# Routing of a token group moved from six steps behind the attention loop to four, and the one-hot weighting moved from GpSimd to VectorE

## What is computed

```python
h = layernorm(x) @ W.T + b_W
e = (h @ a1)[:, None] + (h @ a2)[None, :] + b_a
e = where(e > 0, e, 0.2 * e)
attention = softmax(where(adj > 0, e, -9e15), axis=1)      # 2048 x 2048
x = x + attention @ h
z = layernorm(x)
logits = z @ Wr + br
topk_logits, topk_idx = top_k(logits, 2)
gates = softmax(topk_logits)
out = 0
for e in range(64):
    y = relu(z @ W1[e] + b1[e]) @ W2[e] + b2[e]            # 128 -> 256 -> 128
    out = out + combine[:, e:e+1] * y                      # combine: the gates at topk_idx, 0 elsewhere
x = x + out
```

## Time and profile before

| what | us |
|---|---|
| runs, median of 3 | 335.87 |
| runs, lowest and highest | 334.42 and 335.96 |
| the profiled execution | 333.78 |
| its span, first to last instruction | 332.0 |
| DVE busy | 216.4 |
| PE busy | 223.2 |
| POOL busy | 185.0 |
| ACT busy | 143.9 |

### The profile page before, as it was taken

One profiled execution on the slowest core, in us unless ns is written; L12 is line 12 of the kernel. 1 busy time (PEld: TensorE's weight loads), 2 busy tenths in 40 slices (PEclk: granted clock), 3 DMA queues, 4 the chain that ended last, 5 costly groups with the idle time before them and its releaser, 6 DMA issues.

```text
span 332.0 us, 6227 instructions
## 1 busy us (share of the span) xinstructions
PE 223.2 (67%) x1797; PEld 212.2 (64%) x1797; DVE 216.4 (65%) x583; ACT 143.9 (43%) x313; POOL 185.0 (56%) x210
## 2 busy tenths in 40 slices
PE   0790888999589579793431510209999999999830
PEld 0760788989589478793320410209999989999830
DVE  3859999999999299756734000005666756676476
ACT  1146858888862477632500200015664333444400
POOL 5510068998779867887774777773234323333300
PEclk9997899999989859998555585558999999999995
DMA  6993505998976200010111632213555656664184
GB/s 162 158 183 66 102 0 94 287 248 217 238 197 190 105 17 2 24 34 25 48 48 37 180 88 64 56 40 105 162 155 160 179 147 172 170 178 136 34 243 137
DMA packets 29056, 40.55 MB, mean 122 GB/s; under 512 B 3744, under 2 KB 24416, under 8 KB 28000
## 3 DMA queue, kind: packets, MB, share of 16 engines
q1 hardware_dynamic: 23280, 25.14, 25.7%
q0 software_dynamic: 5376, 14.72, 20.0%
q10 hardware_dynamic: 368, 0.30, 0.5%
HBM read 43.27 MB, written 5.26 MB: 146 GB/s over the span
## 4 chain that ended last, share of the span: by engine, by line
PE 35%; DVE 20%; issue 18%; POOL 14%; DMA 4%; ACT 4%; another core or an unknown queue 4%; SPq 1%; DVEq 0%; POOLq 0%; ACTq 0%
PE bank L907 13%; PE bank L917 13%; POOL table L361 7%; DVE arena L570 6%; DVE xs L753 2%; POOL ve L341 2%; POOL rstd L343 2%; PE bank L785 2%; DMA xs<-in_x 2%; DMA arena<-result 1%; POOL rk L369 1%; PE bank L897 1%; PE bank L822 1%; PE bank L775 1%
## 5 line engine op out<-in xcount | busy, mean ns | idle before, releaser
L907 PE MATMUL bank<-arena 128*128 x380 | 61.4, 287 | 30.3 <-issue 19.8
L907 PEld LDWEIGHTS bank<-arena 128*128 128x128 f32 x380 | 52.2, 200 | 31.7 <-issue 31.5
L407 POOL DMA_INDIRECT result<-arena x32 | 30.8, 963 | 60.8 <-DVE arena L731 55.9
L487 ACT ACTIVATE arena<-bank,arena 128x128 f32<-128x128 f32 x95 | 34.9, 368 | 60.9 <-PE bank L907 31.5
L822 PE MATMUL bank<-arena 128*128 128x130 f32 x512 | 61.3, 278 | 0.0
L822 PEld LDWEIGHTS bank<-arena 128*128 128x128 f32 x512 | 59.9, 194 | 0.0
L917 PE MATMUL bank<-w2s,arena 128*128 x380 | 59.1, 279 | 1.0 <-issue 1.0
L731 DVE SCALAR_TENSOR_TENSOR arena<-bank,arena 128x128 f32 x95 | 33.3, 351 | 39.6 <-PE bank L917 21.8
L812 PE MATMUL bank<-ident,arena 128*128 128x128 f32 x256 | 36.0, 301 | 25.9 <-DVE arena L570 25.4
L724 DVE TENSOR_SCALAR arena<-bank,arena 128x128 f32<-128x128 f32 x95 | 33.1, 348 | 30.2 <-issue 16.1
L917 PEld LDWEIGHTS bank<-w2s,arena 128*128 128x128 f32 x380 | 51.0, 195 | 1.6 <-issue 1.6
(11 more groups left out here) (156 smaller groups left out, 268.8 us busy)
## 6 DMA issues: line engine op xcount, KB each, us to landing
arena<-in_w1b SPq DMA_DIRECT2D x95, 129.0 KB
arena<-in_adj POOLq DMA_DIRECT2D x16, 512.0 KB, 6.9
w2s<-in_w SPq DMA_DIRECT2D x8, 1024.0 KB
arena<-result SPq DMA_DIRECT2D x8, 256.0 KB, 4.4
xs<-in_x SPq DMA_DIRECT2D x4, 256.0 KB, 5.4
out<-xs SPq DMA_DIRECT2D x4, 256.0 KB, 2.3
table<-rows_out,pos POOLq DMA_INDIRECT x32
arena<-table,arena POOLq DMA_INDIRECT x32
```

The costliest lines, as they stand in the source:

```text
L487: act.activation(hT[:, p % UH, 0, :], hp(p, 0), ACT.Relu, bias=w1s[:, p % UW, HID:HID + 1]).then_inc(e_ha, 1)
L907: ins = pe.matmul(hp(p, b), w1s[:, p % UW, P * b:P * b + P], xT_all[:, bass.ds(column, P)], start=True, stop=True)
```

## The change

Five things are altered. (1) The places of the routing in each engine's loop: PE's `route_a` goes from step z+2 behind `attend` to step z+1 ahead of `attend`, `route_b` from z+3 to z+1 behind `attend`, `route_c` from z+4 to z+2; DVE's `top2` from z+5 to z+3 and its `place` from z+6 to z+4; POOL's `counts` from z+5 to z+3, and its scatters from z+6 to z+4 on, with one tile a step for groups 0 and 1 in place of two. (2) ACT's `norm(s-3)` stands ahead of `evac(s-1)` in every step. (3) The groups have 4, 4, 4, 2 and 2 tiles. (4) POOL's `combine` is gone. DVE makes `comb` with 32 operations on 128x64 behind the table's last operation, with one 64-wide half for each of a token's two experts, so that the last transposes and products are 128 deep in place of 64, and `b2` is loaded twice. (5) `up(0)` stands ahead of `take(2)`.

```diff
-    START = [0, 4, 8, 11, 14, T]
+    START = [0, 4, 8, 12, 14, T]
-    SLOT = [0, GRP, 0, 3, 6]
+    SLOT = [0, GRP, 0, GRP, 6]
...
-        combT = carve(N)[0:E, :]
+        combT = carve(N)
+        comb = carve(T * TOPK * E).rearrange("p (t k e) -> p t k e", t=T, k=TOPK)
-        b2_s = sb("b2_s", [E, D])
+        b2_s = sb("b2_s", [TOPK * E, D])
-        idxf = sb("idxf", [P, GRP, TOPK])
+        idxf = sb("idxf", [P, T, TOPK])
...
 # POOL
-            def combine(q):
...
-            for s in range(T + 7):
+            for s in range(T + 5):
                 if 0 <= s - 3 < T:
                     rstd_of(s - 3)
                 if s + 5 < T:
                     load(s + 5)
                 for q in range(NG):
                     z = START[q + 1]
-                    if s == z + 5 and q < COUNTED:
+                    if s == z + 3 and q < COUNTED:
                         counts(q)
                     for j in range(SIZE[q]):
-                        if s == z + 6 + (0 if z > T - 3 else (j + q // 2) // 2):
+                        if s == z + 4 + (j, j, max(0, j - 1), 0, 0)[q]:
                             place(q, START[q] + j)
-                    if q < 2 and s == z + 6:
-                        combine(q)
...
-            for q in range(2, NG):
-                combine(q)
 # ACT
-            for s in range(T + 7):
+            for s in range(T + 4):
                 if s < T:
                     scores(s)
+                if 0 <= s - 3 < T:
+                    norm(s - 3)
                 if 1 <= s <= T:
                     evac(s - 1)
-                if 0 <= s - 3 < T:
-                    norm(s - 3)
                 for q in range(NG):
+                    if s == START[q + 1] + 2:
+                        route_a(q)
                     if s == START[q + 1] + 3:
-                        route_a(q)
-                    if s == START[q + 1] + 5:
                         route_b(q)
 # DVE
                 if q >= 2:
-                    dve.wait_ge(s_comb, min(q - 1, 2))
+                    dve.wait_ge(s_cnt, min(q - 1, 2))
...
-                if 1 <= q <= 2:
-                    dve.wait_ge(s_comb, q)
...
-                    if s == START[q + 1] + 5:
+                    if s == START[q + 1] + 3:
                         top2(q)
-                    if s == START[q + 1] + 6:
+                    if s == START[q + 1] + 4:
                         place(q)
...
             dve.scalar_tensor_tensor(mask, hi, pidx[:, :], above, ALU.is_gt, ALU.mult).then_inc(s_mask, 1)
+            for t in range(T):
+                for k in range(TOPK):
+                    ins = dve.tensor_scalar(comb[:, t, k, :], iota_e, idxf[:, t, k:k + 1], gate[:, k, t:t + 1], ALU.is_equal, ALU.mult)
+            ins.then_inc(s_comb, 1)
 # PE
-            for s in range(T + 7):
+            for s in range(T + 3):
                 if s < T:
                     turn(s)
+                for q in range(NG):
+                    if s == START[q + 1] + 1:
+                        route_a(q)
                 if 1 <= s <= T:
                     attend(s - 1)
                 for q in range(NG):
+                    if s == START[q + 1] + 1:
+                        route_b(q)
                     if s == START[q + 1] + 2:
-                        route_a(q)
-                    if s == START[q + 1] + 3:
-                        route_b(q)
-                for q in range(NG):
-                    if s == START[q + 1] + 4:
                         route_c(q)
...
-            for b in range(3):
-                take(b)
+            take(0)
+            take(1)
             up(0)
+            take(2)
             up(1)
```

More of the change, by code:

```diff
@@ L35, in build @@
     TAB = PACK * WORDS
-    assert TAB <= P and NB <= 32 and E <= 64
+    assert TOPK * E == P and TAB <= P and NB <= 32 and E <= 64
     EPS = 1e-5
@@ L150, in build @@
         gate = sb("gate", [P, TOPK, T])
-        cm = rk
         nm2 = sb("nm2", [P, T])
-        comb = sb("comb", [P, T, E])
         bank = [ctx.enter_context(nc.psum_tensor(f"bank{i}", [P, 512], F32)) for i in range(8)]
@@ L414, in _ @@
             act.dma_start(bss[:, :], biases.to_broadcast([P, D + 1 + E])).then_inc(d_small, 16)
-            act.dma_start(b2_s[:, :], b2).then_inc(d_small, 16)
+            for k in range(TOPK):
+                act.dma_start(b2_s[k * E:(k + 1) * E, :], b2).then_inc(d_small, 16)
             for b in range(4):
@@ L498, in _ @@
                 act.wait_ge(s_ct, q + 1)
-                act.activation(combT[:, START[q] * P:START[q + 1] * P], bank[q][0:E, 0:SIZE[q] * P], ACT.Copy).then_inc(s_cts, 1)
+                act.activation(combT[:, START[q] * P:START[q + 1] * P], bank[q][:, 0:SIZE[q] * P], ACT.Copy).then_inc(s_cts, 1)
         @block.vector
@@ L536, in _ @@
             stats(1)
-            dve.wait_ge(d_small, 16 * 3)
+            dve.wait_ge(d_small, 16 * 4)
             dve.tensor_copy(a2rep[:, :], a_s[:, 1:2].to_broadcast([P, P]))
@@ L595, in top2 @@
                 link(ins)
-                link(dve.tensor_copy(idxf[:, 0:n, :], idx8[:, 0:n, 0:TOPK]))
+                rows = slice(START[q], START[q + 1])
+                link(dve.tensor_copy(idxf[:, rows, :], idx8[:, 0:n, 0:TOPK]))
                 if q >= 2:
-                    dve.wait_ge(s_comb, min(q - 1, 2))
+                    dve.wait_ge(s_cnt, min(q - 1, 2))
                 for k in range(TOPK):
@@ L601, in top2 @@
                                             iota_e[:, :].rearrange("p (g e) -> p g e", g=1).to_broadcast([P, n, E]),
-                                            idxf[:, 0:n, k:k + 1].to_broadcast([P, n, E]), ALU.is_equal)
+                                            idxf[:, rows, k:k + 1].to_broadcast([P, n, E]), ALU.is_equal)
                 link(ins)
@@ L622, in place @@
                 link(dve.tensor_reduce(rank[:, :, 0:n], rk[:, :, 0:n, :], AX.X, ALU.add))
-                link(dve.scalar_tensor_tensor(posf[:, :, 0:n], idxf[:, 0:n, :].rearrange("p g k -> p k g"), float(N),
+                link(dve.scalar_tensor_tensor(posf[:, :, 0:n], idxf[:, rows, :].rearrange("p g k -> p k g"), float(N),
                                               rank[:, :, 0:n], ALU.mult, ALU.add))
@@ L649, in _ @@
             dve.wait_ge(s_pool, 4)
-            for s in range(1, T + 7):
+            for s in range(1, T + 5):
                 if s < T:
@@ L942, in _ @@
             for q in range(NG):
-                pe.wait_ge(s_comb, q + 1)
+                pe.wait_ge(s_comb, 1)
                 for g in range(SIZE[q]):
-                    ins = pe.transpose(bank[q][0:E, P * g:P * g + P], comb[:, START[q] + g, :], ident[:, :])
+                    ins = pe.transpose(bank[q][:, P * g:P * g + P], comb[:, START[q] + g, :, :].rearrange("p k e -> p (k e)"), ident[:, :])
                 ins.then_inc(s_ct, 1)
```

## The result

The changed kernel takes 344.38 us (median of 4 runs, 342.85 to 346.60), the kernel before 335.89 in the runs beside it: a ratio of 1.0263 [1.0232, 1.0294] (the two medians alone give 1.0253). The profiled execution took 344.34 against 333.78. The forecast was 350, range 330 to 358, slower.

The account below looks back on a forecast made before the run. DVE paces the loop at 6.13 us a step, barely ahead of a two-step dependence loop; delaying the first gather delays the end. 2.1 + 6.4 + 13.5 - 6.0 + 3.5 - 3.6 = +15.9 on 333.78: 349.7, said 350, range 330 to 358.

Parts of the forecast that it names:

- the two mechanisms: In the loop: norm ahead of `evac` lengthens plain steps, +6.4; PE waits for the norm ahead of `attend`, +13.5.
- the table: Stretch from the loop's end to the first gather: time left unchanged, 0, with bounds 0 and -8 us.
- First norm: At the first norm, already late, `evac`'s time ahead of the scores counts in full: +2.1 us.
- ACT's order: Norm ahead of `evac` puts `evac` inside the dependence loop: 0.8 us in about eight plain steps, +6.4.
- `route_a` ahead of `attend`: PE waits for the late norm before `attend`, delaying DVE by 2.5, 5.5 and 5.5 us in groups 0 to 2: +13.5.
- `combine` off POOL with spread scatters: In the step at 106.20, weighting and four scatters no longer hold back POOL's chain; L570's wait goes: -6.0 us.
- Third `top2`: With earlier routing a third group's `top2` is paid on DVE within the loop: +3.5 us.
- Behind the last `attend`: Earlier placing of the group on DVE, -2.0, and fewer scatters ahead on POOL, -1.6: together -3.6 us.
- Weights 0: 32 weight operations on DVE, at most 10 us, fit inside 40 us of standstill during the gathers: 0.
- the rival of up to +10: Weight operations on DVE hold up POOL's gathers, moving the last by 6.4 to 10.2 us: 356 to 360; chance 0.08.
- The faster rival: The norm is ready when PE finishes `turn`, so waits at `route_a` vanish and gains stay: 324 to 326; chance 0.20.
- the signs the forecast named: Plain steps over 6.5 us, waits before `route_a` and `residual`, last `attend` ending near 170, first gather near 194.

Follow-up runs that it names:

- the second chip: Changed kernel, unaltered, run again beside the kernel before on another chip (also called the repeat): 345.25 against 334.41 us, ratio 1.0322.
- the spreading: Kernel before with the weighting moved to DVE, plus scatters of groups 0 to 2 spread one tile a step: 329.83 us, ratio 0.9834.
- the weighting alone: Kernel before without POOL's `combine`, 32 weight operations on DVE, `b2` loaded twice, routing still six steps behind: 331.35 us, ratio 0.9900.
- Pacing POOL: Kernel before, with POOL issuing gather b only when PE has taken up block b-6: 327.66 us, ratio 0.9809.

## Why the prediction was right, and where not

The direction, the two mechanisms and their places were right; the time came out 5.6 us under the forecast and in the range. For the profiled execution the forecast was 349.7 against 344.34, and the events of the first table split these 5.4 us: the start +0.9, the loop 17.7 for 19.5, the stretch behind it -4.4 for -3.6, the table -5.0 for 0, the weights' stretch +2.1 for 0 and the end -0.7. By its own steps:

- **First norm, +2.1**: L555 of tile 4 comes at 56.06 for 53.91, of which 0.87 stems from the start: +1.3. It waits 1.76 where it waited 0.50. By this profile the term was 0.8 too large; on the second chip the same distance is 25.60 for 23.10 us, +2.5, so one profile does not settle it.
- **ACT's order, +6.4 (0.8 a step)**: right in kind. It holds 0.9 a step where steps alternate, 6.15 and 7.97. I had ruled out that either length "holds steadily"; they hold by turns. In the whole loop DVE waits 6.4 us for `c_hi`, in four places, for which the two terms had 8.5: only three pairs of steps are plain in the changed kernel. Alone it costs 10.5 us in the kernel before, of which the table of the experiments shows 8.7 from the fourth `leaky` on; that includes the step with `combine`, which waits 7.92 there in place of 5.99.
- **`route_a` ahead of `attend`, +13.5 (2.5, 5.5, 5.5)**: measured waits before `residual` 4.01, 8.21 and 2.38, sum 14.6 (3.89, 7.98 and 2.58 on the second chip). The places and the sum were right, the shares not. Undoing the order gave back only 9 to 11, since part of the wait moved to the logits. Two causes for the shares: PE's clock is at 0.5 for a part of `attend` behind each of the two waits, so `attend` takes 5.29 and 5.76 where I put 3.8 (1.5 and 2.0 us), and in the third group L555 itself came 2.39 late for `c_hi`, which left less to wait behind it. The clock had no term in the working.
- **`combine` off POOL with spread scatters, -6.0**: in that step 2.35 from the weighting and 4.1 more from the spreading, 6.5 together; from the fourth `leaky` to the first gather, 6.6 us together (131.0 to 124.4), of which the weighting alone gives 4.1 (126.9): in that one step it is the smaller part, over the loop the larger one. Right, with both shares.
- **Third `top2`, +3.5**: it stands in the loop now, from 152.71 on, ahead of L555 at 156.11: 3.4. Right.
- **Behind the last `attend`, -3.6**, and the table 0 with bounds 0 and -8: the first was -4.4. **The table was mis-sized**: from PE's counts to the first gather 14.43 us became 9.48, -5.0. I had the possibility as a bound and took none of it; this is the largest error, and accounts for most of the 5.6 us. It was not tried by itself, but the profiles point at the scatters. POOL issues them 1.27 us apart and may gather only when all 32 have landed. In the kernel before nine of them are issued after PE's last counts and the last one ends 11.2 us behind the counts; in the changed kernel it is five and 6.9 us, and from there to the first gather 3.3 and 2.6 us. In all profiles the stretch follows their number (9, 8, 7, 5: 14.3, 13.3, 12.0, about 9 us), and on the chips without the standstill the profile names the landing of a scatter as what the first gather waited for. DVE and PE do the same work there in both kernels, and DVE's wait ahead of L694 (L678 after) is 3.10 before and 1.24 after. By the program it needs only the products up to L887, which had ended 4.3 us earlier at 173.2; what held it back is open.
- **Weights 0, with the rival of up to +10**: the gathers kept their 38.84 us, so that rival falls. By the Trainium skill, "SBUF — State Buffer", section "SBUF: two separate sides", a VectorE operation in a two-port mode keeps GpSimd from writing the descriptors of its transfers, and the prediction took the weights for such operations. No run shows in which mode they ran; 32 of them in a row moved no gather, while the 2.3 us operations made scatters of 0.96 us last up to 2.94. The measurement decides: of the operations seen here only the long ones cost POOL time. But the weights stand ahead of the first `relu`: it comes 10.9 us after the first gather in place of 9.5, and steady work 45.0 in place of 42.9. (The prediction gives this last distance as 39.8; that is the one to the end of the last gather.) On the second chip from the first gather to the end it is 155.0 for 155.5, so this loss is not settled.
- **The start, +0.9**: not in the sum. The chain of the changed kernel begins with the second load of `b2`. It was seen in the repeat (31.11), but not in the kernel with the weighting alone, which loads `b2` twice too (29.95). Open.
- **What the forecast did not see**: the wait of `top2` for the logits. It was hidden in the changed kernel by the two orders, and decides what undoing them is worth. The faster rival, "the early norm is in time", priced 324 to 326 for a kernel without waits at PE; with the orders undone, which comes nearest to it, the ratio is 0.9944 and not 0.97.

Among the signs the forecast named, the last `attend` was to end near 170 and ends at 169.9; the first gather near 194 and came at 187.6, which is the table's 5 us and about 1 between `attend` and the counts.

## What to carry to other kernels

Moving a consumer earlier costs the slack of its whole chain: list every hand-over of that chain (statistics, norm, transpose, copy, product) with its latest row before, and count how many engine turns are left between them; if that is none, there will be a wait, and here an order of the engines that served the chain first cost more than leaving the consumer to wait. Where a small operation is stretched by a long one of another engine, look at where its start falls, not at its length. And a stretch that "stands still anyway" is worth one run that throttles the engine that is busy in it.

## What was unexpected of the hardware

- **The standstill goes with the chip.** The same kernel before takes 304.5 us on two chips and 334 to 336 in three series on at least two others. Each chip was used in one series, so it could also be the series. Up to the first gather the kinds do not differ in the one pair that can be compared (124.4 and 124.5 us in the table of the experiments). In 190 to 220 us, with all gathers back to back, the kernel with both orders undone shows on a chip of the first kind:

```profile
190.00:220.00 30.00, 28.97 (x243) 28.37 (x243) 18.58 (x54) 17.20 (x54) 22.69 (x25) 0.95 0.63 173
```

  against PE 4.75 above. POOL's busy time is the same (22.69 and 23.11), so the gathers take no longer. What differs are the steps of other queues in between; SP's register operations, 0.03 us each in the other profile, reach 0.70 us there:

```profile
L289 SPq MOVE arena<-in_w1b x95: 12/29/702, 180.8 to 304.5; - x95
```

  (ns minimum, median, longest.) Pacing POOL gives back 6.8 of the 30 us. Why some chips do this stays open; a comparison across chips would be off by 10%, more than any effect measured here.
- **PE's clock falls around its waits, and `attend` grows**: after 2.66 us of wait the next `attend` took 5.29 us, after 6.06 us 5.76, against 3.75. The granted clock was 0.5 from 71 to 74 us, when PE was at work again, and from 109 to 115 us, from within the wait on.
- **A scatter's time depends on where it starts**: 0.96 us beside small DVE operations, and 1.8 to 3.2 over all profiles when it starts inside L548 or L555, 0.1 us or more behind the operation's start. One that starts less than 0.05 us behind it, or ahead of it, takes 0.95 to 1.15.
